# Turning the quantised feed-forward rows with transposing DMAs in a one-core decoder layer

## What is computed

```python
def h_bitlinear(x, w):
    return jnp.einsum('bsh,oh->bso', act_quant(fwht(x)), weight_quant(w))
gate = bitlinear(x, w_gate)                      # 512 -> 2048
up = bitlinear(x, w_up)
intermediate = jax.nn.silu(gate) * up
return h_bitlinear(intermediate, w_down)         # 2048 -> 512
```

## Time and profile before

| what | value |
|---|---|
| time, median of 3 runs | 1487.06 us (1485.8 to 1487.59) |
| span of the profiled execution | 1483.3 us |
| TensorE (PE) busy | 1448.3 us, 98% |
| VectorE (DVE) busy | 1091.2 us, 74% |
| ScalarE (ACT) busy | 637.7 us, 43% |
| GpSimd (POOL) busy | 435.9 us, 29% |
| chain of waits that ended last | 85% on PE |
| first `turn_q` in the trace, first `down` | 1281.1 us, 1289.2 us |

### The profile page before, as it was taken

The page is one execution under the profiler, slowest core; times in us unless marked ns, Lnnn a source line. Parts: engine busy times, 40 slices in busy tenths (PEclk is TensorE's granted clock), DMA queues, the critical chain, the costliest instruction groups (busy, mean ns, idle before and its releaser), DMA issues.

```text
span 1483.3 us, 23970 instructions
## 1 busy us (share of the span) xinstructions
PE 1448.3 (98%) x9240; PEld 1167.8 (79%) x9240; DVE 1091.2 (74%) x2062; ACT 637.7 (43%) x1205; POOL 435.9 (29%) x283
## 2 busy tenths in 40 slices
PE   8999999999999999999999999999999999999998
PEld 6888888888888888888888888878888646666675
DVE  5567766666667777777677687688787886977788
ACT  4333333333324333333333334234343466776775
POOL 0311011211205445435554423221421343333320
PEclk9999999999999999999999999999999999999999
DMA  4554433443524444435555311101211225444452
GB/s 158 176 138 128 120 97 104 124 119 94 152 71 136 118 139 132 132 110 130 163 157 165 118 44 51 51 8 36 78 44 35 88 79 184 122 129 144 154 172 92
DMA packets 213297, 166.53 MB, mean 112 GB/s; under 512 B 89664, under 2 KB 174528, under 8 KB 213184
## 3 DMA queue, kind: packets, MB, share of 16 engines
q1 hardware_dynamic: 191920, 133.27, 30.4%
q10 hardware_dynamic: 21264, 31.73, 7.2%
HBM read 115.02 MB, written 49.94 MB: 111 GB/s over the span
## 4 chain that ended last, share of the span: by engine, by line
PE 85%; DVE 7%; DMA 2%; POOL 2%; ACT 2%; issue 1%; SPq 0%; POOLq 0%; ACTq 0%; DVEq 0%
PE bank L490 17%; PE bank L496 17%; PE bank L493 17%; PE bank L723 6%; PE bank L618 4%; PE bank L738 4%; PE bank L759 3%; PE bank L580 2%; PE bank L553 2%; PE bank L604 2%; DVE AM L1198 1%; PE bank L575 1%; PE bank L561 1%; PE bank L588 1%; DVE OKM L1176 1%
## 5 line engine op out<-in xcount | busy, mean ns | idle before, releaser
L490 PE MATMUL bank<-Wh,X 128*128 128x512 f32 x512 | 205.6, 402 | 0.1
L496 PE MATMUL bank<-Wh,X 128*128 128x512 f32 x512 | 200.0, 391 | 0.0
L493 PE MATMUL bank<-Wl,X 128*128 128x512 f32 x512 | 199.3, 389 | 0.0
L490 PE MATMUL bank<-X,Wh 128*128 128x512 f32 x384 | 156.4, 407 | 6.3 <-ACT Wh L816 6.3
L1512 POOL TENSOR_TENSOR Wl<-RAW,Wh 128x512 fp32r<-128x512 f32 (+1 forms) x65 | 112.1, 1734 | 135.9 <-ACT Wh L816 135.8
L496 PE MATMUL bank<-X,Wl 128*128 128x512 f32 x384 | 150.8, 393 | 0.0
L493 PE MATMUL bank<-X,Wh 128*128 128x512 f32 x384 | 150.2, 391 | 0.0
L1535 POOL TENSOR_TENSOR sm<-sm,half 128x8 f32<-128x8 f32 x31 | 51.0, 1647 | 328.1 <-DVE sm L1223 328.1
L1558 POOL TENSOR_TENSOR LO<-M,HI 128x512 fp32r<-128x512 f32 x64 | 82.6, 1291 | 160.3 <-PE bank L732 128.0
L878 ACT ACTIVATE V<-bank 128x256 f32<-128x256 f32 x128 | 48.7, 381 | 182.1 <-PE bank L496 181.8
L723 PE MATMUL bank<-XT,W 128*128 128x512 bf16 x512 | 121.9, 381 | 0.6 <-DVE GS L1381 0.6
(11 more groups left out here) (223 smaller groups left out, 3280.9 us busy)
## 6 DMA issues: line engine op xcount, KB each, us to landing
z_scratch<-EV SPq DMA_DIRECT2D x64, 256.0 KB, 2.0
Z<-z_scratch SPq DMA_DIRECT2D x16, 1024.0 KB, 5.8
o_scratch<-OG ACTq DMA_DIRECT2D x96, 128.0 KB, 2.4
AM<-o_scratch ACTq DMA_DIRECT2D x24, 512.0 KB, 4.7
RAW<-wgT SPq DMA_DIRECT2D x16, 512.0 KB, 4.6
RAW<-wuT SPq DMA_DIRECT2D x16, 512.0 KB, 4.4
RAW<-wdT SPq DMA_DIRECT2D x16, 512.0 KB, 4.4
RAW<-Wo SPq DMA_DIRECT2D x14, 512.0 KB, 4.4
```

Source lines behind the costliest of these rows:

```text
L490: engine.matmul(o, lh(c), rh(c), start=c == 0, stop=False)
L493: engine.matmul(o, lh(c), rl(c), start=False, stop=False)
L496: last = engine.matmul(o, ll(c), rh(c), start=False, stop=c == n - 1)
```

## The change

TensorE no longer transposes `HQ`. In its place ScalarE, at the stage `turn_q` (place 4i+31), waits for each half of `HQ` and for `down` of the tile before, and issues a transposing DMA from `HQ` to `HT` for it, 128x1024 bf16 (256 KB) each. `down` waits for these DMAs (`hq_in0`, `hq_in1`) in place of the two copies, and `clamp` waits for the DMAs of the tile before in place of TensorE's transposes. The stage `turn_q_out` with ScalarE's and VectorE's copies is gone, and so are the two banks per tile. Nothing else of the order is changed.

```diff
-        38), ("low", 2), ("turn_q_out", 32), ("had2_out", 24), ("high", 2), ("round", 29), ("gs", 0), ("add", 35),
+        38), ("low", 2), ("had2_out", 24), ("high", 2), ("round", 29), ("gs", 0), ("add", 35),
...
-            def ffn_tile(stage, i):
-                if stage == "turn_q":
-                    for k in range(2):
-                        bk = take(("hq", i, k), (S[f"hq_evac{k}"], i + 1))
-                        pe.wait_ge(S["hq_made"], 2 * i + k + 1)
-                        v = bk[:].bitcast(BF).rearrange("p (c t) -> p c t", c=8)
-                        for c in range(8):
-                            mm = engine.transpose(v[:, c, :], HQ[:, 1024 * k + 128 * c:1024 * k + 128 * c + 128], IDB[:])
-                        mm.then_inc(S["hq_turned"], 1)
...
-                            pe.wait_ge(S[f"hq_evac{j // 8}"], i + 1)
+                        pe.wait_ge(S[f"hq_in{j // 8}"], 16 * (i + 1))
...
-                elif stage == "turn_q_out":
-                    i = n
-                    act.wait_ge(S["hq_turned"], 2 * i + 1)
-                    act.wait_ge(S["down"], i)
-                    engine.activation(HT[:, 0:8, :], bank("hq", i, 0)[:].bitcast(BF).rearrange("p (c t) -> p c t", c=8),
-                                      ACT.Copy).then_inc(S["hq_evac0"], 1)
+                elif stage == "turn_q":
+                    for k in range(2):
+                        act.wait_ge(S["hq_made"], 2 * n + k + 1)
+                        act.wait_ge(S["down"], n)
+                        engine.dma_start_transpose(HT[:, 8 * k:8 * k + 8, :], HQ[:, 1024 * k:1024 * k + 1024]
+                                                   ).then_inc(S[f"hq_in{k}"], 16)
...
-                        dve.wait_ge(S["hq_turned"], 2 * i)
+                        dve.wait_ge(S[f"hq_in{h}"], 16 * i)
...
-                elif stage == "turn_q_out":
-                    dve.wait_ge(S["hq_turned"], 2 * i + 2)
-                    dve.wait_ge(S["down"], i)
-                    engine.tensor_copy(HT[:, 8:16, :], bank("hq", i, 1)[:].bitcast(BF).rearrange(
-                        "p (c t) -> p c t", c=8)).then_inc(S["hq_evac1"], 1)
```

More of the change, by code:

```diff
@@ L193 @@
 UNIT = (("absmax", 25), ("had1_out", 5), ("read", 20), ("gate", 0), ("clamp", 30), ("h", 1), ("scale", 28), ("store",
-        38), ("low", 2), ("turn_q_out", 32), ("had2_out", 24), ("high", 2), ("round", 29), ("gs", 0), ("add", 35),
+        38), ("low", 2), ("had2_out", 24), ("high", 2), ("round", 29), ("gs", 0), ("add", 35),
         ("had1", 4), ("normal", 37), ("turn_q", 31), ("had2", 23), ("down", 33), ("silu", 0))
-TILES = {"read", "scale", "round", "clamp", "turn_q_out", "add", "normal", "store", "turn_q", "down"}
+TILES = {"read", "scale", "round", "clamp", "add", "normal", "store", "turn_q", "down"}
 HOLD = (('o', 12), ('en', 13), ('y', 7), ('vg', 9), ('xm', 11), ('gate', 7), ('up', 8), ('h1', 7), ('h2', 8), ('down', 11), ('hq', 6), ('xt', 10), ('q', 10), ('k', 9), ('s', 8), ('sc', 14), ('wt', 7), ('ok', 14), ('okt', 8), ('w', 7), ('ot', 9), ('kt', 4), ('et', 5), ('hk', 7), ('hv', 9), ('att', 12), ('x1', 11), ('qk', 11), ('spread', 12))
@@ L236 @@
 gate up gs_made h_silu h_made h_hi h_lo had1 h1_evac z_out0 z_out1 z_in0 z_in1 had2 h2_evac h_absmax h_scale f_made
-h_round hq_made hq_turned hq_evac0 hq_evac1 down ffn_add n3_moments n3_var n3_rstd n3_applied
+h_round hq_made hq_in0 hq_in1 down ffn_add n3_moments n3_var n3_rstd n3_applied
 """.split()
@@ L740, in ffn @@
                     mm.then_inc(S["had2"], 1)
-                elif stage in ("turn_q", "down"):
-                    ffn_tile(stage, n)
-            def ffn_tile(stage, i):
-                if stage == "turn_q":
-                    for k in range(2):
-                        bk = take(("hq", i, k), (S[f"hq_evac{k}"], i + 1))
-                        pe.wait_ge(S["hq_made"], 2 * i + k + 1)
-                        v = bk[:].bitcast(BF).rearrange("p (c t) -> p c t", c=8)
-                        for c in range(8):
-                            mm = engine.transpose(v[:, c, :], HQ[:, 1024 * k + 128 * c:1024 * k + 128 * c + 128], IDB[:])
-                        mm.then_inc(S["hq_turned"], 1)
-                elif stage == "down":
[L754 to L757, removed]
-                            pe.wait_ge(S[f"hq_evac{j // 8}"], i + 1)
[L759 to L771, removed]
@@ new lines, in ffn, with down @@
+                elif stage == "down":
+                    down(n)
+            def down(i):
+                bk = take(("down", i), (S["ffn_add"], i + 1))
+                pe.wait_ge(S["w3_in2"], 16 * 4)
+                if i < 15:
+                    for j in range(16):
+                        pe.wait_ge(S[f"hq_in{j // 8}"], 16 * (i + 1))
+                        mm = engine.matmul(bk[:], HT[:, j, :], WD[:, j, :], start=j == 0, stop=j == 15)
+                    mm.then_inc(S["down"], 1)
+                else:
+                    halves = (bk, take(("down", 16), (S["ffn_add"], 17)))
+                    for js, cols, bh in [(js, cols, bh) for js in (range(8), range(8, 16))
+                                         for cols, bh in zip(COLUMNS, halves)]:
+                        pe.wait_ge(S[f"hq_in{js[0] // 8}"], 16 * (i + 1))
+                        for j in js:
+                            mm = engine.matmul(bh[:, cols], HT[:, j, :], WD[:, j, cols], start=j == 0, stop=j == 15)
+                        if js[0]:
+                            mm.then_inc(S["down"], 1)
@@ L1393, in ffn @@
                                          apply_absolute_value=True).then_inc(S["h_absmax"], 1)
-                elif stage in ("scale", "clamp", "turn_q_out", "add", "normal"):
+                elif stage in ("scale", "clamp", "add", "normal"):
                     ffn_tile(stage, n)
```

## The result

The changed kernel takes 1501.7 us (median; 1499.6 to 1502.7) against 1486.4 us before: 1.0105 times as long, 95% interval 1.0094 to 1.0117. Forecast were 1481.7 us and faster. Its profiled execution has a span of 1497.8 us, 14.5 more than before.

The account below looks back on a forecast made before the run. TensorE, without idle time in the steady feed-forward part, was taken to bound the kernel. The terms -8.8 + 0.8 - 0.3 + 2.9 = -5.4 us gave 1481.7 us; the forecast's own range was 1479.5 to 1484, the whole range 1476.5 to 1512.

Parts of the forecast that it names:

- part 1: Tiles 0 to 8, among the gate steps: TensorE saves 0.98 us of transposes per tile, 8.8 us gained.
- part 4: Tiles 9 and 10, inside the wait for tile 12's read: no gain; shared engines cost that read 0.8 us.
- part 5: Tiles 11 to 13: the DMA's latency replaces the transposes almost evenly, -0.1 us per tile, -0.3 in all.
- part 6: Tiles 14 and 15: HT's single buffer makes tile 15's DMA wait for the down before; 2.9 us lost.
- Part 2: Price of a transposing DMA: first half lands 2.9 us after issue, second 4.1, within the cover of tiles 0 to 8.
- x: Transfer time of one 256 KB transposing DMA, without its fixed latency; taken as 1.2 us.
- rival A: Transposing DMA as quick as a plain copy, landing in 2.0 to 2.2 us: 9.6 us gained, 1477.5 us; chance 0.08.
- Part 3: ScalarE and VectorE: two issues, 0.9 us, replace 1.02 us of ScalarE copies per tile; silu 0.4 us late, covered.
- Rival D: Each issue blocks ScalarE 2 us or more, TensorE waits about 1.5 us per tile; 1498 us; chance 0.07.
- The clock: Named way to be wrong: the granted clock, 1.00 in all these stretches, falls in the new waits; no size given.
- the formula: Tiles 11 to 13 each change by the first half's landing minus 3.0 us; the end by twice it minus 2.9.
- C: Turned side written in short pieces, transfers well above 2.1 us, tail down waits for second half; 1497.7 us; chance 0.25.

Follow-up runs that it names:

- e1: Kernel before, with transposing DMAs for tiles 0 to 8 only and TensorE transposing tiles 9 to 15; 1480.4 us, ratio 0.9966 to before.
- e2: Kernel before, with transposing DMAs for tiles 9 to 15 only and TensorE transposing tiles 0 to 8; 1508.4 us, ratio 1.0155 to before.
- e7: Changed kernel with one transposing DMA of 128x2048 (512 KB) per tile in place of two of 128x1024; 1510.8 us, ratio 1.0168 to before.
- e8: Kernel before, with transposing DMAs for tiles 0 to 7 only and TensorE transposing tiles 8 to 15; 1477.1 us, ratio 0.9943 to before.
- e3: Changed kernel reading only one sixteenth of Z for tiles 12 to 15, that part of the computation left out; 1485.3 us, ratio 1.000 to before.
- e5: Changed kernel with extra idle matmuls in TensorE's long waits of the tail; 1495.8 us, ratio 1.0067 to before.
- its control: Kernel before, reading only one sixteenth of Z for tiles 12 to 15; 1485.1 us, ratio 1.000 to before.

## Why the prediction was wrong

**What bounds the kernel, and part 1: right.** 3.08 us for the place of `turn_q`, 8.5 us for nine tiles where the sum had 8.8. e1 and e2 show the gain apart from the rest.

The sum by its terms, in us, from the distances between like starts in the two traces:

| term | forecast | measured | of it slow matmuls |
|---|---|---|---|
| part 1, nine tiles | -8.8 | -8.5 | |
| part 4, last `had1` to `down` of tile 10 | +0.8 | +6.8 | 1.6 |
| part 5, `down` of tile 10 to that of tile 13 | -0.3 | +11.2 | 4.2 |
| part 6, `down` of tile 13 to the last | +2.9 | +5.0 | 1.7 |

**Part 2: the price alone was near, the price in company was the mistake.** I put x at 1.2 us and the landing of the first half at 2.9, 0.4 of it for sharing the engines. Alone it is 2.73 / 2 = 1.37 and 3.3: the packet was priced well (60.7% x 4.5 x 16 / 2112 = 20.7 ns for 19 ns), the fixed part is 2.0 us and not 1.3. Beside a read of `Z` the pair's median landing is 6.3 us, and `down` of tile 11 could not start before 1448.9, 6.8 us after the issue at 1442.1. The term of 0.4 is the step that failed most: 3.0 to 3.5 us stand in its place (6.3 and 6.8 against 3.3). It needed no new hardware fact: 3.9 us of reading and storing and 2.5 us of transposing take about their sum. And it was readable that they fly together: in the kernel before, the read goes out when TensorE ends the same `had2` whose copy ScalarE makes just ahead of its `turn_q`. The mean share of the engines in the tail (0.31, rows 1), which rival A took for idle engines, says nothing of that moment: it is 1 MB at full rate and then nothing, and the DMAs start with the megabyte. The Trainium skill's "DMA: Bandwidth & Descriptors" (section Latency and other measured facts) gave an estimate of 1.0 us for 256 KB, at 261 GB/s; e7 shows 1.3 us. The Trainium skill's 1309 ns for one 128x128 block by DMA ("VectorE: DVE Perf Modes", section The three transpose paths) does not hold for a block among many: here eight took 1.37 us.

**Part 3: right in its result among the gate steps, wrong in a number, and wrong behind them.** An issue holds ScalarE's queue for 1.35 us, not for the 0.46 of a plain DMA, 2.7 us per tile. In the gate stage `silu` is some 1.3 us late and nothing follows from it. Behind the last gate step the copies out of PSUM that stand behind it do count; I had named them and let them cost nothing. Rival D's price, 1.5 us of waiting per tile, did not come; its mechanism did for tiles 8 and 9, and is in part 4.

**Part 4: the term of 0.8 us stood for the wrong cost.** Sharing cost the read of tile 12 nothing (6.7 us to land in both kernels; the slowest read, 10.0 us, is that of tile 13, for which TensorE did not wait). But it goes out 4.8 us later, so that TensorE's `had2` of tile 12 starts 1432.77 - 1417.7 = 15.1 us behind the last `had1` in place of 1436.45 - 1426.2 = 10.3, and 2.0 more are lost up to `down` of tile 10, 1.6 of them by the clock. Four kernels part the 4.8 us. The read goes out 3.35 us behind the last `had1` in e8, 5.5 in e1 (with tile 8's DMAs), 6.0 in e2 (with tile 9's) and 8.2 in the changed kernel: 2.1 us for tile 8, 2.6 for tile 9. Tile 9's issues stand right ahead of the last copy to `EV`. Tile 8's hold an earlier copy for 1.3 us (1412.46 in e1, 1411.13 in e8). The read of tile 11 then also goes out 1.3 us later, the store behind it lands after 6.7 us in place of 5.3, and the next but one copy waits for that store. The two stores beside tile 8's DMAs themselves land after 2.2 and 2.8 us, against 2.0 and 2.7. So it is ScalarE's queue and not the shared engines, as far as these traces tell; no run issued the DMAs from another queue.

**Parts 5 and 6: the formula was right for what it was given.** With a landing of 3.3 us it says 0.3 per tile for 11 to 13; without reads (e3) a tile took 8.02 for 7.97 us, because ScalarE comes to the issue 1.15 us after `down` (1428.38 - 1427.23) and not 1.53. In the changed kernel the distances from `down` to `down` of tiles 10 to 13 are 11.4, 12.9 and 10.8 us, 11.2 us more than 3 x 7.97. At the end, from `down` of tile 13 to that of tile 15, it is 1489.06 - 1472.58 = 16.5 for 1474.58 - 1463.12 = 11.5 us, the latter from this line of the kernel before:

```profile
1463.12 3.62 PE L759 MATMUL bank<-W,HT 128*128 128x512 bf16 x16
```

2 x 3.3 - 2.9 = 3.7 of the 5.0 are the formula's, the rest is the slower `down` of tile 14.

**The clock.** I named it as a way to be wrong and priced it at nothing. Three `down` products at half the clock for part of their length take 5.9 us more than 3.6 each, one group of `had2` 1.6; e5 gets 4.4 to 5.9 us back by idle work alone. That it fell is shown by the rows; how much of the remaining tail is its share and how much the transfers' cannot be parted exactly, because each changes the other.

The account of the tail's 22.9 us by e3 and its control: without the reads the changed tail is 59.7 against 50.8, so 8.9 us are left when nothing collides with a read. 2.0 of them lie ahead of tile 9's `down`, 5.1 between `down` of tile 13 and the last one, and 1.7 in the last `down` at a low clock. The other 22.9 - 8.9 = 14.0 us are what full reads add: the collision with them, the clock that falls in its waits, and the late start of the read of tile 12, which costs only if the read is long. e3 does not part the last from the first.

**The rivals.** C is nearest in time (1497.7 us) and in place (the nine tiles keep their gain, the tail loses it), with another cause: the transfers are not slow by their pieces, they share, and `down` waits for the first half already. That its number came near is luck. Had I put its mechanism as "the DMA and the read fly together, and the work of both has to be done", its price would have been in the rows.

## What to carry to other kernels

An engine's instruction can be traded for a DMA where there is cover between issue and use, measured in that stage: 7.9 us among the gate steps held, 3 us in the tail did not, and the best kernel (e8, 0.57% faster than before) makes the trade in the one stage only. For a transfer's landing, add up what is in flight with it at that moment, not the mean share of the engines in the stretch. An issue that is put into an engine's queue delays what stands behind it by its own length: look at the last copy that a read waits for, not only at the steady stage. A wait that is new on TensorE is to be priced with the slower matmuls behind it.

## What the runs showed of the hardware

An issue of a transposing DMA holds the issuing queue the longer the larger it is: 1.35 us for 128x1024 and 2.39 us for 128x2048 bf16 in the median, where a plain one took 0.46. With reads in flight it holds it longer, up to 3.96 us for one of 256 KB in the changed kernel. A transposing DMA of 256 KB lands 3.3 us after issue when alone, 1.3 us more than a plain store of 256 KB in packets of 2 KB. Issued beside a 1 MB read it lands after 6.3 us in the median. Behind four of the five waits of 3.45 to 4.41 us in the changed kernel TensorE's granted clock was at half for part of the next group; behind the last, 3.45 us ahead of the last `down`, it was not (3.65 us). Idle matmuls in these waits kept it up (e5); one fall remained, at tile 10, behind a wait of 2.64 us that had none.
